# Expert tiles of 18 instead of 21, the upper half of each split into two quarters of 32 rows

## The reference

```python
logits = xt @ gate_w.T                       # 592 x 15
scores = softmax(logits)
topk_w, topk_idx = top_k(scores, 3)          # 3 of 15 experts for each token
topk_w = topk_w / (sum(topk_w) + 1e-20)
h = einsum('td,efd->etf', xt, fc1_w) + fc1_b # 2 x 256 wide for each expert
xh, g = h[..., :256], h[..., 256:]
a = gelu(g) * xh * geglu_mult
yexp = einsum('etf,edf->etd', a, fc2_w) + fc2_b
y = einsum('etd,te->td', yexp, comb)         # comb: the three weights, else 0
# plus the shared expert, 512 wide, for every token; then the residual and a layer norm
```

## Time and profile before

| what | us |
|---|---|
| median of 3 runs | 211.79 |
| the profiled execution | 211.57 |
| its span in the trace | 209.8 |
| TensorE busy | 199.2 (95%) |
| VectorE busy | 113.2 (54%) |
| GpSimd busy | 121.5 (58%) |
| ScalarE busy | 94.4 (45%) |

### The profile page before, as it was taken

The page is one execution under the profiler, slowest core; times in us unless marked ns, Lnnn a source line. Parts: engine busy times, 40 slices in busy tenths (PEclk is TensorE's granted clock), DMA queues, the critical chain, the costliest instruction groups (busy, mean ns, idle before and its releaser), DMA issues.

```text
span 209.8 us, 4431 instructions
## 1 busy us (share of the span) xinstructions
PE 199.2 (95%) x1559; PEld 124.7 (59%) x1559; DVE 113.2 (54%) x313; ACT 94.4 (45%) x219; POOL 121.5 (58%) x148
## 2 busy tenths in 40 slices
PE   7999998999998899999998999999999999999981
PEld 4776676678786675776775753355444555445630
DVE  6685697868863444264799953642344332231034
ACT  2004565477868373564557762333332433235024
POOL 0040079869989857929999877216665552347100
PEclk9999999999999999999999999999999999999996
DMA  6999999960000399922220034228985321112483
GB/s 199 391 416 314 402 415 417 425 270 0 6 3 3 97 379 376 417 83 64 78 71 22 0 100 108 78 92 304 366 326 164 92 75 53 50 50 91 145 248 116
DMA packets 13822, 38.32 MB, mean 183 GB/s; under 512 B 2697, under 2 KB 4618, under 8 KB 13802
## 3 DMA queue, kind: packets, MB, share of 16 engines
q1 hardware_dynamic: 11786, 32.54, 42.4%
q0 software_dynamic: 2016, 5.51, 8.4%
HBM read 29.27 MB, written 4.06 MB: 159 GB/s over the span
## 4 chain that ended last, share of the span: by engine, by line
PE 77%; DVE 8%; DMA 6%; issue 2%; ACT 2%; POOL 2%; SPq 1%; POOLq 0%; DVEq 0%; ACTq 0%
PE ps L383 66%; PE ps L1874 3%; PE ps L1672 2%; DMA wres<-y_dram 2%; PE ps L1914 2%; PE ps L1687 2%; DMA embed_sb<-embed 1%; POOL y_dram L668 1%; DMA embed_sb<-x_dram,gather_i 1%; DMA y_dram<-ln_mem,dest_i 1%; PE ps L1603 1%; PE ps L1530 1%; DVE over L1270 1%; POOL embed_sb L659 1%; ACT ln_mem L905 1%
## 5 line engine op out<-in xcount | busy, mean ns | idle before, releaser
L383 PE MATMUL ps<-wres,cT 128*64 (+1 forms) x360 | 63.1, 469 | 0.0
L383 PEld LDWEIGHTS ps<-wres,cT 128*64 128x64 f32 (+1 forms) x360 | 25.4, 131 | 27.7 <-issue 20.5
L668 POOL DMA_INDIRECT y_dram<-ln_mem,dest_i x21 | 20.6, 982 | 26.8 <-ACT ln_mem L875 23.4
L426 POOL TENSOR_TENSOR wres<-wres,fac_mem 128x512 f32<-128x512 f32 x22 | 27.2, 1271 | 4.3 <-DVE ln_rs L1033 4.3
L659 POOL DMA_INDIRECT embed_sb<-x_dram,gather_i x21 | 20.3, 968 | 8.2 <-issue 5.2
L1406 DVE TENSOR_TENSOR fac_mem<-ps,h 128x256 f32<-128x256 f32 x21 | 8.9, 423 | 24.0 <-ACT h L869 24.0
L869 ACT ACTIVATE h<-ps 128x256 f32<-128x256 f32 x21 | 8.0, 383 | 28.5 <-PE ps L383 28.5
L383 PE MATMUL ps<-h,stage 128*128 128x296 f32 x64 | 18.2, 422 | 0.7 <-DVE xn L1384 0.6
L1413 DVE COPY cT<-ps 128x256 f32<-128x256 f32 x21 | 8.8, 424 | 15.6 <-PE ps L383 15.6
L875 ACT ACTIVATE ln_mem<-ps 128x256 f32<-128x256 f32 x21 | 8.0, 383 | 15.8 <-PE ps L383 15.8
L383 PEld LDWEIGHTS ps<-h,stage 128*128 128x128 f32 x64 | 11.6, 190 | 5.4 <-DVE xn L1384 1.0
(11 more groups left out here) (215 smaller groups left out, 379.9 us busy)
## 6 DMA issues: line engine op xcount, KB each, us to landing
wres<-experts SPq DMA_DIRECT2D x15, 768.0 KB, 13.5
fac_mem<-experts SPq DMA_DIRECT2D x11, 256.0 KB, 8.1
wres<-ut SPq DMA_DIRECT2D x3, 768.0 KB, 8.8
embed_sb<-embed SPq DMA_DIRECT2D x5, 416.0 KB, 5.6
stage<-shared SPq DMA_DIRECT2D x2, 771.0 KB, 16.4
stage<-wres SPq DMA_DIRECT2D x2, 512.0 KB
wres<-y_dram SPq DMA_DIRECT2D x2, 512.0 KB, 4.2
wres<-y_dram SPq DMA_DIRECT2D x2, 384.0 KB, 6.3
```

The costliest lines, as they stand in the source:

```text
L383: return nc.tensor.matmul(o, w, x, start=start, stop=stop)
L426: nc.gpsimd.tensor_tensor(w1(e, c), w1(e, c), row, ALU.subtract).then_inc(less_done, 1)
L668: pool.indirect_dma_start(out=y_dram[:, :], out_offset=bass.IndirectOffsetOnAxis(ap=dest_i[:, column(i):column(i) + 1], axis=0), in_=ys[:, ...
```

## The change

Tiles are planned in quarters of TQ = 32 rows: 1761 // 32 + 15 = 70 quarters, so NT = 18 tiles. The first 32 rows of each expert go to its fixed quarter. What exceeds them goes, as far as there are pairs of quarters, to lower halves (64 rows, one expert, by register, as before), and an odd quarter to one of NB = 19 copied quarters. The upper half of a tile is two quarters side by side, partitions 64 to 95 and 96 to 127, each with weights of its own: quarters 0 to 18 are copies, 19 to 33 the fixed experts 0 to 14. So a tile has, for each chunk, one product of 64 weight columns and two of 32. The copied quarters make up columns 0 to 9 of the table (NPAIR = 10). Each even quarter is copied by SyncE's DMA and each odd one by VectorE (`first_copied` for W1, two copies of 128x512; `second_copied` for W2, one copy), into three buffers in turn for W1 and four for W2; a buffer is filled again once the tile that used it has been multiplied. The tiles run in the order COLUMNS: four without copies, then columns 0, 14, 1, 15, 2, 16, 3, 17, then 4 to 9. `slots` gets more steps on VectorE, `owners` fewer elements, `owners_copied` is new. The stretch of SyncE's queue that stores the combine weights is untouched. Cut to its core:

```diff
 BIG = 3e38
 
 
-TM = 64
-PT = P // TM
-NT = ((T * TOPK - E) // TM + E + PT - 1) // PT
+TM, TQ = 64, 32
+PT, PQ = P // TM, P // TQ
+
+QUARTERS = (T * TOPK - E) // TQ + E
+NT = (QUARTERS + PQ - 1) // PQ
 NTT = NT * PT
+
+NB = max(QUARTERS - E - PT * NT, E)
+NPAIR = (NB + 1) // 2
+assert NB + E <= PT * NT
 SUMS = 32
 PC = P // SUMS
...
-NCOPY = NT - E
-NOVER = NTT - E
-RT_END = 28
+COLUMNS = (10, 11, 12, 13, 0, 14, 1, 15, 2, 16, 3, 17, 4, 5, 6, 7, 8, 9)
+assert sorted(COLUMNS) == list(range(NT))
+AT = [COLUMNS.index(n) for n in range(NPAIR)]
...
         yr = wres[:, 0:YC * D].rearrange("p (c d) -> p c d", c=YC)
 
...
+            return COLUMNS[i]
 
...
             sp.wait_ge(st_comb, 64)
             sp.dma_start(comb17[:, :], comb_dram[:, 0:T]).then_inc(ld_c17, 16)
 
-            sp.wait_ge(own_done, 1)
+            sp.wait_ge(own_done, 2)
             all_scaled(sp)
-            for k in range(NCOPY):
-                e = sp.value_load(owner_i[0:1, NT + k:NT + k + 1], min_val=0, max_val=E - 1)
-                sp.wait_ge(f1_mm, 2 * k + 1)
-                sp.dma_start(copy_w1[k], wres[:, bass.ds(e * WC, W1C)]).then_inc(ld_copy, 16)
-                sp.dma_start(copy_w2[k], wres[:, bass.ds(e * WC + W1C, W2C)]).then_inc(ld_copy, 16)
+            sp.wait_ge(f1_mm, 1)
+            copied = {}
+
+            def copy_first(n):
+                e = sp.value_load(owner_i[0:1, NT + 2 * n:NT + 2 * n + 1], min_val=0, max_val=E - 1)
+                if n >= W1_PAIRS:
+                    sp.wait_ge(f1_mm, AT[n - W1_PAIRS] + 1)
+                sp.dma_start(copy_w1[2 * (n % W1_PAIRS)], wres[:, bass.ds(e * WC, W1C)]).then_inc(ld_cw1[n % W1_PAIRS], 16)
+                copied[n] = e
+
+            def copy_second(n):
+                if n >= W2_PAIRS:
+                    sp.wait_ge(y2_mm, AT[n - W2_PAIRS] + 1)
+                sp.dma_start(copy_w2[2 * (n % W2_PAIRS)], wres[:, bass.ds(copied[n] * WC + W1C, W2C)]) \
+                    .then_inc(ld_cw2[n % W2_PAIRS], 16)
+                del copied[n]
+
+            for n in range(NPAIR):
+                copy_first(n)
+                if 0 < n < NPAIR - 2:
+                    copy_second(n - 1)
+            copy_second(NPAIR - 3)
+            copy_second(NPAIR - 2)
+            copy_second(NPAIR - 1)
 
...
+                nc.vector.tensor_tensor(rank[:, :], rank[:, :], flat, ALU.mult).then_inc(rt, 1)
 
...
+                nc.vector.tensor_scalar(over_i[:, 0], posn[:, TT * E:], 1.0, -1.0, ALU.max, ALU.add).then_inc(rt, 1)
+                nc.vector.tensor_scalar(over_i[:, 2], over_i[:, 0], TQ.bit_length() - 1, 1,
+                                        ALU.arith_shift_right, ALU.bitwise_and).then_inc(rt, 1)
+                nc.vector.tensor_copy(counts, over_i[:, 1:3]).then_inc(rt, 1)
+                nc.vector.tensor_tensor_scan(upto.rearrange("p v e -> p (v e)"), rte[:, C_RESET:C_RESET + 2 * E],
+                                             counts.rearrange("p v e -> p (v e)"), 0.0, ALU.mult, ALU.add).then_inc(rt, 1)
+                nc.vector.tensor_scalar(least, counts[:, 0], float(TM), TQ - 0.5, ALU.mult, ALU.add).then_inc(rt, 1)
+                nc.vector.tensor_scalar(pairs2[:, :], upto[:, 0, E - 1:E], float(NT), 2.0, ALU.max, ALU.mult).then_inc(rt, 1)
+                nc.vector.tensor_tensor(odd_t[:, :].rearrange("p (t e) -> p t e", t=TT), places,
+                                        least.unsqueeze(1).to_broadcast([P, TT, E]), ALU.is_gt).then_inc(rt, 1)
+                nc.vector.scalar_tensor_tensor(odd_far, upto[:, 0], -2.0, before[:, 1], ALU.mult, ALU.add).then_inc(rt, 1)
+                nc.vector.tensor_scalar(odd_far, odd_far, pairs2[:, 0:1], float(TQ), ALU.add, ALU.mult).then_inc(rt, 1)
-                nc.vector.tensor_tensor(jump[:, :], slot[:, :], flat, ALU.mult).then_inc(rt, 1)
+                                        odd_far.unsqueeze(1).to_broadcast([P, TT, E]), ALU.mult).then_inc(rt, 1)
+                nc.vector.tensor_tensor(slot[:, :], slot[:, :], odd_t[:, :], ALU.add).then_inc(rt, 1)
...
+            def owners_copied():
+
+                nc.vector.tensor_scalar(ends[:, 0], upto[:, 0], 2.0, None, ALU.mult).then_inc(rt, 1)
+                nc.vector.tensor_tensor(owner_b[:, :, :],
+                                        ends.rearrange("p v e -> p (v e)").unsqueeze(1).to_broadcast([P, NB, 2 * E]),
+                                        rte[:, C_TILE + NT:C_TILE + NT + NB].unsqueeze(2).to_broadcast([P, NB, 2 * E]),
+                                        ALU.is_le).then_inc(rt, 1)
+                dve.wait_ge(rt, 39)
+                nc.vector.tensor_reduce(owner_f[:, NT:], owner_b[:, :, :], AX.X, ALU.add).then_inc(rt, 1)
...
                     softmax_start()
+                if k == 7:
+                    owners_copied()
...
                     ALU.mult).then_inc(mix_done, 1)
 
+            def first_copied(n):
+
+                if n == 0:
+                    dve.wait_ge(own_done, 2)
+                    all_scaled(dve)
+                e = dve.value_load(owner_i[0:1, NT + 2 * n + 1:NT + 2 * n + 2], min_val=0, max_val=E - 1)
+                dve.wait_ge(f1_mm, AT[n - W1_PAIRS] + 1 if n >= W1_PAIRS else 1)
+                for c in range(DC):
+                    nc.vector.tensor_copy(copy_w1[2 * (n % W1_PAIRS) + 1][:, c * 2 * F:(c + 1) * 2 * F],
+                                          w1(e, c)).then_inc(cw1_done, 1)
+                odd[n] = e
+
+            def second_copied(n):
+
+                if n >= W2_PAIRS:
+                    dve.wait_ge(y2_mm, AT[n - W2_PAIRS] + 1)
+                nc.vector.tensor_copy(copy_w2[2 * (n % W2_PAIRS) + 1],
+                                      wres[:, bass.ds(odd[n] * WC + W1C, W2C)]).then_inc(cw2_done, 1)
+                del odd[n]
+            def copies(turn):
+
+                if turn < 4:
+                    first_copied(turn)
+                if 1 <= turn <= 4:
+                    second_copied(turn - 1)
...
                     gated(i)
                 for i in range(max(j - 2, 0), j):
                     gated_in(i)
+                copies(j // 2)
                 if j == 0:
                     softmax_end()
...
                 yield slice(0, TM), w1(lower[i], c)
-                yield slice(TM, P), w1(i, c) if i < E else copy_w1[i - E][:, c * 2 * F:(c + 1) * 2 * F]
+                n = column(i)
+                for h in range(PT):
+                    v = PT * n + h
+                    yield slice(TM + TQ * h, TM + TQ * (h + 1)), \
+                        copy_w1[2 * (n % W1_PAIRS) + h][:, c * 2 * F:(c + 1) * 2 * F] if v < NB else w1(min(v - NB, E - 1), c)
 
...
+                if n < NPAIR:
+                    pe.wait_ge(ld_cw1[n % W1_PAIRS], 16 * (n // W1_PAIRS + 2))
+                    if PT * n + 1 < NB:
+                        pe.wait_ge(cw1_done, DC * (n + 1))
                 if i == 0:
...
+                    if PT * n + 1 < NB:
+                        pe.wait_ge(cw2_done, n + 1)
                 if i >= 2:
                     pe.wait_ge(ys_done, i - 1)
...
                     gated_transposed(i)
                 for i in range(max(j - 4, 0), max(j - 2, 0)):
                     second(i)
+            second(NT - 4)
+            gated_transposed(NT - 2)
+            second(NT - 3)
             gated_transposed(NT - 1)
-            second(NT - 3)
             second(NT - 2)
             second(NT - 1)
```

More of the change, by code:

```diff
@@ L243, in vit_tower_kernel @@
         rank = sb("rank", [P, TT * E])
-        over = sb("over", [P, 5, E])
-        over_i = sb("over_i", [P, E], I32)
+        over = sb("over", [P, 11, E])
+        over_i = sb("over_i", [P, 3, E], I32)
+        pairs2 = sb("pairs2", [P, 1])
+        odd_t = sb("odd_t", [P, TT * E])
         slot = sb("slot", [P, TT * E])
@@ L308, in column @@
         def column(i):
[L310 removed]
+            return COLUMNS[i]
         ps = ctx.enter_context(nc.psum_tensor("ps", [P, 8, 512], F32))
[L315 to L316 removed]
+        ld_chunk = [sem(f"ld_chunk_then_copy{k}") for k in range(KP + 1)]
+        ld_emb, ld_pt = ld_chunk[0:KP], ld_chunk[KP]
         ld_cst, ld_vec, ld_out = sem("ld_cst"), sem("ld_vec"), sem("ld_out_w")
@@ L889, in _ @@
                     tile_out(i)
-            for i in range(NT - 3, NT):
+            for i in range(NT - 4, NT):
                 tile_out(i)
@@ L1254, in reduce_pick @@
                                         AX.X, ALU.add).then_inc(done, 1)
+            counts, upto, before, ends = (over[:, i:i + 2] for i in (0, 2, 4, 6))
+            far, odd_far, least = (over[:, i] for i in (8, 9, 10))
             def slots():
-                held, extra, upto, before, far = (over[:, i] for i in range(5))
                 posn = ps[:, 3, 0:(TT + 1) * E]
+                places = posn[:, 0:TT * E].rearrange("p (t e) -> p t e", t=TT)
                 dve.wait_ge(pos_mm, 1)
-                nc.vector.tensor_scalar(over_i[:, :], posn[:, TT * E:], float(TM - 1), None, ALU.add).then_inc(rt, 1)
```

(33 more changed lines are left out.)

111 lines of the change are left out of this document (65 added, 46 removed).

## The result

The changed kernel takes 274.88 us (median of 4 runs, 273.84 to 276.10) against 212.04 for the kernel before in the same comparison: 1.296 times as long (interval 1.288 to 1.303). The forecast was 215.8; the first rival, products of two widths taking turns, had said 277 with a chance of 0.27.

What follows compares the result with a forecast made beforehand. TensorE bounds the tiles, then GpSimd's scatters; VectorE's routing and first gathers come before. 211.57 - 9.45 (fewer tiles) + 1.3 (routing) + 10.2 (stand) + 2.0 (clock) = 215.6, plus 0.22 to the median: 215.8 us; range 212 to 278, its own 213 to 220.

Steps and rivals of the forecast that it cites:

- the first rival: TensorE products: 64 and 32 columns take turns, emptying TensorE between; 6.9 us a tile, 277 us in all; chance 0.27.
- side by side: TensorE products: one 64-column and two 32-column products run together, so a tile keeps its 3.17 us.
- Fewer tiles: Tile loop and scatters: three tiles go, so the last scatter starts at 184.15 instead of 193.60, a gain of 9.45 us.
- Routing: VectorE's work up to the gather indices: added operations delay the first gather by 1.3 us (0.7 to 3.5).
- the dependent rows: VectorE routing: the profile's price for operations that wait on each other, 0.25 us (75 wide) or 0.2 (small) each.
- `owners_copied` was hidden: VectorE between the last shared unit and `gated(0)`: its 2.4 us fit into idle time and cost nothing.
- The stand at `first(4)`: TensorE at the first copied tile: waits 10.2 us (9.3 to 10.8) for copies queued behind the combine weights' stores.
- The clock: TensorE after that wait: products run at half speed at 1.2 GHz, costing 2.0 us (1.5 to 2.5).
- The bound from the start of the run: Clock's low end, 1.5 us: first twelve 296-column products take 3.14 us, 0.26 each against 0.13 later.
- Later copies in time: Copies after the first pair, by SyncE and VectorE: they arrive before their tiles need them, no cost, little to spare.
- The sum itself: Whole kernel: the profiled execution's time with all terms added, 215.6 us, assuming a tile keeps its 3.17 us.

Runs made afterwards that it cites:

- b_mixed: Kernel before (21 tiles, no new copies), each upper half's 64-column product issued as two of 32 with the same weights; 285.65 us against 213.63.
- all32_order_fixed: Changed kernel with only 32-column products, first copies ahead of the combine weights' stores, lower half on fixed weights without register reads; 203.17 us, ratio 0.957.
- all32: Changed kernel with each lower half's 64-column product issued as two of 32, the second with a fixed expert's weights; 224.23 us, ratio 1.050.
- order: Changed kernel, widths still mixed, with SyncE issuing the first copies ahead of the combine weights' stores; 265.37 us.
- all32_order: Changed kernel with only 32-column products (second lower quarter on fixed weights) and first copies ahead of the combine weights' stores; 204.76 us, ratio 0.962.
- b_all32: Kernel before with four 32-column products per chunk instead of two of 64, rows 32 to 63 on a fixed expert's weights; 219.39 us, ratio 1.027.
- b_all32_fixed: Kernel before with four 32-column products per chunk, all on fixed experts' weights and no expert number read into a register; 211.56 us, ratio 0.998.

## Why the forecast was wrong, step by step

- **"I take 'side by side'"** failed. This is the step: the sum used 3.17 us for a tile, the kernel took 6.76 (13.49 for two). b_mixed shows it alone. I had priced the failure nearly right (6.9 a tile, 277) and gave it a chance of 0.27, because the changes of width on record in the trace of before were between products that want the same columns. What should have weighed more is what TensorE's weight loads do there in the trace of before, a row that I did not show:

```profile
150.06 0.42 PEld L1874 LDWEIGHTS ps<-cst_sb,embed_sb 128*128 128x128 f32 x4 [0.81 <-issue]
```

  The first 128-column weights are loaded at 150.06, when the first transpose starts, and not ahead of it. The evidence I put against it, that four 32s run side by side, is about one width and says nothing on two. That 277 comes so near to 274.9 is in part luck: it had 2.5 us too much for the tiles and 1.3 for the routing, and 0.5 too little for the stand and 1.0 for the clock. The Trainium skill's sentence (TensorEngine Tiling (Array Packing), Key Properties), that changing the mode drains the TensorE, fits the runs, with 128x64 and 128x32 as two modes; the measured price is 0.27 us for a change and back, beside the lost overlap.
- **Fewer tiles, 9.45 us:** nearly right. In the profiled execution of all32_order_fixed, where the first gather is issued at 119.08 (before at 119.14), the last scatter starts at 185.10, against 193.60 before: 8.5 us. Of the 1.0 missing, 0.7 is that `second(12)` ends at 177.81 and not at 177.09 (0.4 of it a wait of `first(4)` for ScalarE's copy), and 0.2 that the last scatter comes late after the one ahead of it:

```profile
185.10 0.97 POOL L702 DMA_INDIRECT y_dram<-ln_mem,dest_i  x1 [0.54 <-ACT ln_mem L909]
```

  That 211.8 - 9.45 + 0.7 gives 203.1 for the 203.2 measured is luck: the 0.7 is not routing, as the next point shows, and about as much was lost elsewhere.
- **Routing, 1.3 us:** nothing measured. From the scan that begins the ranking (`rank`) to the issue of the first gather, in the kernel before and in the changed one:

```profile
105.11 0.57 DVE L1206 TENSOR_TENSOR_SCAN rank<-rte,mask 128x75 f32<-128x75 f32 x1
119.14 1.17 POOL L659 DMA_INDIRECT embed_sb<-x_dram,gather_i  x1 [0.47 <-DVE gather_i L1351]
```
```profile
105.86 0.58 DVE L1239 TENSOR_TENSOR_SCAN rank<-rte,mask 128x75 f32<-128x75 f32 x1
119.81 1.18 POOL L692 DMA_INDIRECT embed_sb<-x_dram,gather_i  x1 [0.37 <-DVE gather_i L1418]
```

  That is 14.03 against 13.95 us; the other runs of the changed kernel give 13.93 to 13.95, those of the kernel before 14.03 to 14.04. The 0.7 by which the first gather is later stands already at the scan, ahead of all that the change does, and this start moves nearly as much among profiled executions of the kernel before's own routing (105.11 to 105.71). So the 0.7 in the expectations of all32 and all32_order_fixed is a late start of one execution. In the routing, the product `rank` x mask was slow (1.12 us), others were faster than the dependent rows, and the 1.21 of L1270 went. `owners_copied` was hidden, as said.
- **The stand at `first(4)`:** place, cause and end right, and `order` shows them: 6.5 us in the changed kernel, for which the rival had 6. In the forecast's own setting (one width) it had 10.2, and all32 measured 11.7. `first_copied(0)` held `combT` by 1.5 us instead of 2.1, as the copies within SBUF are faster than the one out of PSUM that I took:

```profile
134.32 0.42 DVE L1475 TENSOR_TENSOR fac_mem<-ps,h 128x256 f32<-128x256 f32 x1 [3.91 <-ACT h L902]
135.46 0.76 DVE L1511 COPY stage<-wres 128x512 f32 x2 [0.71 <-issue]
```

  That is 0.38 for 512 columns against 0.69 in the earlier trace rows. But the stores took 3.6 us to land, not 3.1, and the copy 3.6, not 2.7; why, I did not separate.
- **The clock, 2.0 us:** 3.0 in the changed kernel (2.85 by the chains: the 24 records of `first(4)` and `first(5)` take 10.79 us there and 7.94 in `order`), 2.5 in all32. The bound from the start of the run was too low. Its 0.13 for a 296-column product does not stand in the earlier trace rows, which have 0.42 for two.
- **Later copies in time:** right but for 0.2 us in all32_order, where TensorE waited for one of VectorE's copies.
- **The sum itself**, 215.6 for a profiled execution of one width: that of all32 took 224.08, 8.5 more. The longer stand is 1.5 of this, the clock 0.5, `first(3)` behind `gated` 2.0 and the gaps 3.6; the first gather was only 0.8 later, not 1.3, which takes off 0.5. The 1.4 left are not split further. So even with the failed step mended, the forecast would have been low by more than its own bounds, and more than half of the miss, the 2.0 and the 3.6, goes with TensorE's late signals, of which it knew nothing.

What stays open: the cause of the gaps inside the products of all32 and b_all32. They need register reads or register-addressed products (b_all32_fixed has neither) and yet are absent in all32_order, which has both and differs only in the order of SyncE's queue. They go with late signals of TensorE, for which the profile names no reason.

## What to carry to other kernels

Before a product is split into narrower ones, look whether all products that are meant to share the array keep one width: a mixture here cost the whole overlap plus 0.27 us for each change and back, while four 32s in place of two 64s cost nothing where no expert number was read into a register. And when a load gets an earlier user, follow its whole queue: a small store ahead of it, and the wait for that store, decided 9.5 us. And before a later start is put down to an edit, look whether it is there already ahead of the edit.

## What the runs showed of the hardware that I had not expected

- 64-column and 32-column products on different columns of the array never overlapped in any round; the change there and back took 0.27 us (1.99 against 4 x 0.43).
- TensorE's clock stayed at 1.2 GHz for 5.95 us of unbroken products after a stand of 6.5 us, and 4.9 us after one of 11.7.
- Issuing the copies in another order took gaps of some 1 us a round out of TensorE's products, with no wait between the two that the profile shows (7.4 us for two tiles in all32, 6.32 in all32_order).
- With the gaps, TensorE's semaphore signals came up to 3.1 us after the products that give them (all32, b_all32), and without them within hundredths.
